# A graph network's node stage: rows normalised in groups of 1, 3, 3 and 3 tiles in place of 3, 3 and 4

## The reference, cut to what matters

```python
x = x + segment_mean_part(layernorm(x))          # L0_gnn
x = x + ffn_top2_of_8(layernorm(x))              # L0_ffn
x = x + gnn(layernorm(x), edge_attrs, edges)     # L1_gnn
x = x + ffn_top2_of_8(layernorm(x))              # L1_ffn
```

## Time and profile before

| what | us |
|---|---|
| median of three runs | 1435.25 |
| the profiled execution, its own time | 1440.99 |
| its span, first to last instruction | 1439.1 |
| PE / DVE / ACT / POOL busy | 1353.6 / 1151.2 / 1003.0 / 922.4 |
| node stage, first statistics to last product | 801.3 to 825.3 |
| first edge weights on PE (line 1741) | 833.2 |
| mean granted TensorE clock | 0.975 |

### The profile page before, as it was taken

How to read it: one execution, slowest core, us unless ns; L and a number is a source line. 1 busy time by engine, 2 the same in 40 slices (tenths; PEclk the granted TensorE clock), 3 DMA queues, 4 the chain that set the end, 5 groups by cost and what they waited for, 6 DMA issues and landing times.

```text
span 1439.1 us, 24478 instructions
## 1 busy us (share of the span) xinstructions
PE 1353.6 (94%) x8774; PEld 833.0 (58%) x8774; DVE 1151.2 (80%) x1459; ACT 1003.0 (70%) x2000; POOL 922.4 (64%) x762
## 2 busy tenths in 40 slices
PE   4957999999899999999999699999999999998999
PEld 3454746888378874888567534434444443336887
DVE  7888927999089972999459769999999999995665
ACT  6237726888178863888457459999999999884433
POOL 4226675888888888888883467777777777762000
PEclk9859999999999999999999999999999999999999
DMA  9429476277827566765622769989999999985421
GB/s 331 155 92 334 134 243 239 37 272 278 294 34 282 187 232 187 281 215 158 182 62 49 238 189 306 306 296 307 309 305 303 307 307 293 294 291 176 144 89 59
DMA packets 91601, 316.54 MB, mean 220 GB/s; under 512 B 23754, under 2 KB 25988, under 8 KB 80859
## 3 DMA queue, kind: packets, MB, share of 16 engines
q1 hardware_dynamic: 45832, 202.57, 37.7%
q0 software_dynamic: 45648, 112.41, 28.7%
HBM read 378.96 MB, written 77.16 MB: 317 GB/s over the span
## 4 chain that ended last, share of the span: by engine, by line
PE 70%; DVE 11%; DMA 8%; POOL 5%; issue 4%; ACT 1%; SPq 0%; DVEq 0%; POOLq 0%; ACTq 0%
PE pair L1599 32%; PE pair L1741 7%; PE pair L1636 4%; PE pair L1761 4%; DMA arena<-node_table,arena 4%; POOL arena L1953 4%; DVE arena L1048 3%; PE pair L1758 3%; PE pair L1855 3%; PE pair L1866 3%; PE pair L1653 3%; PE pair L1703 2%; PE pair L1590 2%; POOL pair_rows L1906 1%; DVE arena L1045 1%
## 5 line engine op out<-in xcount | busy, mean ns | idle before, releaser
L1916 POOL DMA_INDIRECT sorted_edges<-arena x311 | 460.1, 1480 | 104.2 <-issue 96.0
L910 DVE TENSOR_TENSOR weights_hl<-arena,weights_hl 128x1024 fp32r<-128x1024 f32 x342 | 405.3, 1223 | 62.3 <-ACT weights_hl L1242 59.7
L1953 POOL DMA_INDIRECT arena<-node_table,arena x352 | 340.7, 968 | 129.6 <-issue 89.4
L1242 ACT ACTIVATE weights_hl<-arena 128x1024 fp32r<-128x1024 f32 x342 | 351.9, 1060 | 46.6 <-PE pair L1599 46.4
L1599 PE MATMUL pair<-weights_hl,rows_hl 128*128 128x512 f32 x1368 | 325.9, 395 | 4.3 <-ACT weights_hl L1242 3.0
L1048 DVE TENSOR_TENSOR arena<-pair,arena 128x1536 f32<-128x1536 f32 x176 | 307.7, 1748 | 0.0
L1599 PEld LDWEIGHTS pair<-weights_hl,rows_hl 128*128 128x128 f32 x1368 | 251.7, 188 | 69.8 <-DVE weights_hl L910 10.5
L1741 PE MATMUL pair<-arena 64*128 64x512 f32 x704 | 185.3, 634 | 7.2 <-DVE arena L1048 7.0
L1599 PE MATMUL pair<-weights_hl,hidden_hl 128*128 128x512 f32 x684 | 165.7, 395 | 0.0
L1391 ACT ACTIVATE arena<-arena 128x32 f32<-128x32 bf16 x704 | 157.8, 314 | 0.0
L1045 DVE TENSOR_TENSOR arena<-pair,arena 128x512 f32<-128x512 f32 x176 | 120.8, 686 | 29.5 <-PE pair L1741 19.8
(11 more groups left out here) (292 smaller groups left out, 1541.0 us busy)
## 6 DMA issues: line engine op xcount, KB each, us to landing
arena<-in_w SPq DMA_DIRECT2D x73, 2048.0 KB, 8.6
arena<-in_w SPq DMA_DIRECT2D x85, 1024.0 KB, 9.2
sums<-arena SPq DMA_DIRECT2D x88, 512.0 KB, 5.7
other_down<-in_w SPq DMA_DIRECT2D x8, 1024.0 KB, 12.2
arena<-in_v SPq DMA_DIRECT2D x16, 512.0 KB, 4.6
pair_rows<-arena SPq DMA_DIRECT2D x1, 5934.0 KB, 26.2
arena<-pair_rows SPq DMA_DIRECT2D x23, 256.0 KB, 3.9
arena<-node_table,arena POOLq DMA_INDIRECT x352
```

Source lines behind the costliest of these rows:

```text
L910: v.tensor_tensor(out=part[s][:, 1], in0=by_chunk(n)[4], in1=part[s][:, 0].bitcast(F32), op=ALU.subtract).then_inc(v_low, 1)
L1242: a.activation(out=part[s][:, 0], in_=cols, func=ACT.Copy).then_inc(a_high, 1)
L1916: g.indirect_dma_start(out=sorted_edges, out_offset=bass.IndirectOffsetOnAxis(ap=slot_i[:, j:j + 1], axis=0), in_=er[:, j, :], in_offset=N ...
L1953: g.indirect_dma_start(out=row, out_offset=None, in_=table, in_offset=bass.IndirectOffsetOnAxis(ap=senders[:, i:i + 1], axis=0)).then_inc( ...
```

## The change

The groups become 1, 3, 3 and 3 tiles. There is one group more, and so one more `variance`, one more `root` and one more `scales`. ScalarE's list is written anew to go with it; the wait of `apply_node` asks for the group that its tile is in. Nothing else differs.

```diff
-NORMS = (range(0, 3), range(3, 6), range(6, NT))
+NORMS = (range(0, 1), range(1, 4), range(4, 7), range(7, NT))
@@
             def apply_node(t):
-                a.wait_ge(v_scale, (t // 3 if t < 6 else 2) + 4)
+                a.wait_ge(v_scale, [t in group for group in NORMS].index(True) + 4)
@@
             root(NORMS[0])
             apply_node(0)
+            root(NORMS[1])
+            copy_node(0)
             apply_node(2)
-            copy_node(0)
-            root(NORMS[1])
             copy_node(1)
             copy_rows(0)
-            apply_node(4)
+            root(NORMS[2])
             copy_node(2)
             copy_rows(1)
+            apply_node(4)
             copy_node(3)
             copy_rows(2)
-            root(NORMS[2])
+            apply_node(6)
             copy_node(4)
             copy_rows(3)
-            apply_node(6)
+            root(NORMS[3])
             copy_node(5)
             copy_rows(4)
             apply_node(8)
```

## The result

The kernel after took 1439.36 us (median of nine runs, 1435.3 to 1443.2) against 1435.4 (nine runs, 1431.41 to 1439.07): a ratio of 1.0032, 95% interval 1.0016 to 1.0047. That is 4.6 us slower, 2.3 to 6.8. I had forecast no change, 1435.5 us, with 1438.0 as the upper end.

What follows compares the result with a forecast made beforehand. PE was taken as the bound, busy 94% of the span, so only the node stage's end counted: 2.05 us won on tile 0, lost in later waits, net +0.2, 1435.25 + 0.2 = 1435.5 us; range 1433.3 to 1438.0.

Steps and rivals of the forecast that it cites:

- The start: Node stage start: tile 0 turned 2.05 us earlier, then a wait of about 3 us for tile 1, losing 0.9.
- slow first epsilon: DVE's first epsilon, node stage: priced at 0.69 to the next start, where others take 0.27.
- The middle: Node stage, tiles 2 to 6: PE waits 1.0 us for tile 4; turn 6 comes at 818.5, as before.
- The end: Last group: reciprocal 818.15, shift usable 819.35, turn 7 at 820.35 against 820.01; stage ends 825.45 against 825.33.
- The root behind a row copy: ScalarE's list, last group: root(3) stands behind rows(3), so it starts at 817.9 though possible at 817.4.
- The clock: Rival, node stage: PE's clock rises later, at 814.5 for +0.7 or 818 for +1.6, 1436.2 to 1437.1; chance 0.24.
- Order of the lists: Node stage, walk of the engines' lists: 825.1 before and 825.3 after, taken as +0.2 us; forecast's chance 0.52.
- slower by over 0.2%: Whole kernel: outcome fed by the low clock and part of the edge-stage rival; chance 0.06.
- a clock that stays low to the end: Rival, node stage: low clock kept through both gaps to tile 7 and beyond, +3.0 to +4.4, 1438.3 to 1439.7; chance 0.04.
- a loss in the edge stage: Rival, edge stage: its 88 steps fall into another rhythm, some us either way, 1432 to 1438; chance 0.08.

Runs made afterwards that it cites:

- e5: Kernel after, unchanged, profiled and timed a second time: stage 26.9 us, ratio to the kernel before 1.0032.
- e9: Kernel after with root(3) moved ahead of copy_node(4) and copy_rows(3) in ScalarE's list: stage 26.1 us, ratio to the kernel before 1.0001.
- the five profiles: Profiles of the kernel after and its variants in which GpSimd's packing copies are free; the collision is in all of them.
- e1: Kernel after with GpSimd's six packing copies held back until the last normed tile: stage 24.2 us, ratio to the kernel before 0.9992.
- e8: Kernel before, unchanged, for a second profile: stage 24.0 us.
- e2: Kernel before with GpSimd's packing copies held back until the last normed tile: stage 23.8 us, ratio 1.000.
- e4: Kernel before with eight extra GpSimd copies run over the last scales block: stage 26.6 us, ratio 1.0025.
- e7: Kernel before with groups of 3, 4 and 3 tiles, ScalarE's list reordered and packing copies held back: stage 23.6 us, ratio 1.0005.
- e10: Kernel before with groups of 3, 4, 3, reordered ScalarE list, held copies and 20 filler products in place of 11 ahead of the first turn: stage 23.2, ratio 0.9996.

## Why the prediction was wrong, point by point

- **The start: right.** First turn forecast at t = 4.4, measured 4.0 (the slow first epsilon, 0.59, did not recur: 0.15); second turn forecast 8.4, measured 8.1, with PE waiting 3.00 us for tile 1. The 2 us won on tile 0 did become a wait for tile 1.
- **The middle: a gap too many.** A wait of PE of 1.0 us ahead of tile 4's turn was forecast. There was next to none: PE was at the low clock to t = 11.2 (13.7 in e5) and came late itself. It made no difference to the end: turn 6 came at t = 17.0, forecast 17.2.
- **The end: the step that failed.** "Reciprocal 818.15, shift usable 819.35" priced the last scales block at its usual 0.98 (and 0.20 until its result can be used) while the next sentence let GpSimd's copies run from 818.12 on, and charged them only to the normed tile (0.95 against 0.55). The row at 818.25 was the only slow one that I had put down to a copy, and I read it as a price of that operation, not of the neighbour. Measured: 3.17 for the block (2.8 in e9), 2.2 us more. Of these, 0.3 came back because the reciprocal started earlier than forecast (t = 16.6 against 16.9) and 0.4 because the first normed tile of the last group, behind the copies, paid nothing: turn 7 came at t = 20.6 in place of the forecast 19.1. The copies also began earlier, at t = 15.3 to 16.2 in place of 16.85: GpSimd waited 10.6 to 11.1 us for the records in the five profiles, 11.8 in both of the kernel before. Why they land earlier was not tried.
- **The root behind a row copy: right**, and covered once the copies are away (e1).
- **The clock: a rival, at another place and priced alone.** It stood at +0.7 to +1.6 for a later rise. That came in e5: a rise at t = 13.7, near the 13.2 that the forecast priced at +0.7, and a root 1.0 later than in the first profile. In the first profile it fell behind the gap at tile 7, for 1.6 us. The Trainium skill (TensorE: Matmul & The Clock Gate, section HAM oscillation) says that short groups of work with waits between them can throttle the engine again; the waits of its example are longer than the one here. This trace agrees as to the effect (2.04 us of gap, then 0.50), and e5, with 2.00 and no fall, shows that it is not so every time.
- **The sum.** Order of the lists +0.1 to +0.4 (forecast +0.2); collision with what follows from it +2.7 to +3.4 (27.6 and 26.9 against 24.2 in e1). In all the stage is 2.9 us longer (e5 against e8) to 3.5 (the first two profiles), within the measured 2.3 to 6.8. The medians stand 4.6 us apart, and where the further 1 to 2 us lie stays open, and whether they exist. The profiles can't tell: the edge stages of the kernel after, 478.2 and 480.0 us, are shorter than those of the kernel before, 480.6 and 483.4, but both profiled executions of the kernel before (1440.99 and 1440.97) lay some 5 us above the medians of their kernel, and of the kernel after one (1435.3) was the fastest of its nine and the other (1440.4) lay at the median.
- **The chances.** 0.06 for slower by over 0.2% was too little, and it stood on other mechanisms, a clock that stays low to the end and a loss in the edge stage. Missing was the step of holding a piece of work that moves by a microsecond against every neighbour that it moves beside.

## What to carry to other kernels

When a change moves a block of small operations in time, list what the *other* engines do at the new place, and charge a neighbour's slow-down to every operation beside it, not to the one that happened to show it. A chain of six tiny dependent operations is a bad place for it: each can be held up by nearly a whole copy of another engine (0.75 of 0.8 us here). A packing step with slack behind it can be held by a wait on a semaphore until such a chain is through; here that cost nothing that a timing could show (e1, e2).

## What the runs showed of the hardware that I had not expected

An operation of DVE on 128x3 or 128x4 numbers takes 0.16 us alone and 0.60 to 0.76 when it starts early in a GpSimd copy of 128x704 or 128x352 words (0.8 us each); the later in the copy it starts, the less it takes (0.52, 0.33, 0.25). The ends show what lies behind these numbers: in e4 and in the five profiles with the collision every one of the slow small operations ends 0.01 to 0.03 us behind the end of a copy. So these were held until the copy was through. Hit were products of two SBUF operands, the shift, which also reads two (line 992), an operation with one SBUF source and two constants (line 468), the epsilon (line 478, 0.60) and normed tiles. Not hit were the statistics (0.69 to 0.70 in all runs) and their aggregates (0.18), the reciprocal (0.18 with a copy beside it and without), and the table rows of line 978, whose source is PSUM (0.69 beside the copies in e1).

The Trainium skill (GPSIMD Engine Reference, Specifications) says that GpSimd's SBUF interfaces are shared with VectorE and that it contends with VectorE instructions with two SBUF inputs or in a two-port mode. The runs agree with this for the products and the shift and put a number to it: up to 4.8 times the duration for the smallest operations (0.76 against 0.16). In which mode the operations with one source ran no view shows. GpSimd's copies took 2.98 us for four in the kernel after, beside the small operations, and the same when held back; beside normed tiles of 128x512 they took longer, 3.19 in the kernel before and 3.39 in e4.

The trace of the kernel before held a first sign of this, ahead of the forecast: its slow first epsilon (804.24, 0.59) ends at 804.83, and GpSimd's write of edge records beside it at 804.85:

```profile
803.67 1.18 POOL L1930 DMA_INDIRECT sorted_edges<-arena  x1 [0.30 <-issue]
```

In all six profiles whose first group has three tiles (before, e2, e4, e7, e8, e10) the first epsilon, 0.25 to 0.59 long, ends 0.02 to 0.04 us ahead of the end of such a write. Products of two operands ran beside the same writes at 0.16 (805.93 and 806.13 in the kernel before), and so did the epsilon of a group of one tile (0.15). No run moved these writes, so this rests on the rows alone. I had taken the 0.69 to the next start as a fixed price of the first epsilon, and not asked what stood beside it.
